# The scan's sums in fp16 high and low parts, and the group norm's centring in the summing matrix

## The reference, cut to what matters

```python
def step(S, inp):
    r_t, k_t, v_t, w_t = inp
    o_t = jnp.einsum('bhk,bhkv->bhv', r_t, S) + jnp.einsum('bhk,hk,bhk,bhv->bhv', r_t, u, k_t, v_t)
    S = jnp.exp(w_t)[..., None] * S + k_t[..., :, None] * v_t[..., None, :]
    return (S, o_t)
...
_, o = jax.lax.scan(step, S0, xs)
mean = o.mean(-1, keepdims=True)
var = o.var(-1, keepdims=True)
o = ((o - mean) * jax.lax.rsqrt(var + EPS)).reshape(B, T, VAL_DIM)
o = (o * gn_w + gn_b) * (g * jax.nn.sigmoid(g))
return o @ W_o
```

## Time and profile before

| | |
|---|---|
| median of 3 runs | 1851.65 us |
| lowest, highest | 1848.84, 1853.36 us |
| span of the profiled execution, first to last instruction | 1847.4 us |
| start of the scan's first product | 1714.6 us |
| start of the first gated product (L1738) | 1794.34 us |
| PE, DVE, ACT, POOL busy over the span | 94%, 78%, 76%, 77% |

### The profile page before, as it was taken

One profiled execution on the slowest core, in us unless ns is written; L12 is line 12 of the kernel. 1 busy time (PEld: TensorE's weight loads), 2 busy tenths in 40 slices (PEclk: granted clock), 3 DMA queues, 4 the chain that ended last, 5 costly groups with the idle time before them and its releaser, 6 DMA issues. The chain is left out here.

```text
span 1847.4 us, 53971 instructions
## 1 busy us (share of the span) xinstructions
PE 1740.1 (94%) x22856; PEld 1101.7 (60%) x22856; DVE 1444.6 (78%) x2658; ACT 1407.5 (76%) x1737; POOL 1430.4 (77%) x851
## 2 busy tenths in 40 slices
PE   5999999999999999999999999986899999978997
PEld 2466666666666666666666666675556666653454
DVE  5888888888888888888888887535988888845785
ACT  2688888888888888888888888943998888853463
POOL 6699999999999999999999999974765566624122
PEclk9899999999999999999999999998999999989998
DMA  5101010111101010101010010050111111110000
GB/s 142 25 20 31 19 31 23 27 26 28 26 24 30 21 31 19 31 23 28 23 31 23 24 26 4 2 165 18 41 40 36 37 37 37 34 26 1 1 0 24
DMA packets 71080, 56.89 MB, mean 31 GB/s; under 512 B 29196, under 2 KB 64184, under 8 KB 70840
## 3 DMA queue, kind: packets, MB, share of 16 engines
q1 hardware_dynamic: 70840, 53.44, 11.5%
HBM read 14.54 MB, written 1.05 MB: 8 GB/s over the span
## 5 line engine op out<-in xcount | busy, mean ns | idle before, releaser
L278 POOL TENSOR_TENSOR ah_probs_lo<-ah_probs,ah_probs_hi 128x1024 f16<-128x1024 f32 x512 | 1072.8, 2132 | 78.8 <-ACT ah_probs L487 78.7
L542 DVE TENSOR_REDUCE ah_part_max<-ah_p_m 128x1 f32<-128x512 f32 x1024 | 669.2, 685 | 120.9 <-PE ah_p_m L342 111.1
L484 ACT ACTIVATE ah_probs_hi<-ah_p_s 128x1024 f16<-128x1024 f32 x512 | 531.2, 1038 | 190.0 <-PE ah_p_s L358 178.8
L487 ACT ACTIVATE ah_probs<-ah_p_s 128x1024 f32<-128x1024 f32 x512 | 532.4, 1040 | 0.0
L372 PE MATMUL ah_p_o<-ah_v_hi,ah_probs_hi 128*128 128x65 f16 x4096 | 470.5, 195 | 5.7 <-POOL ah_probs_lo L278 5.1
L374 PE MATMUL ah_p_o<-ah_v_lo,ah_probs_hi 128*128 128x64 f16 x4096 | 470.5, 193 | 0.0
L376 PE MATMUL ah_p_o<-ah_v_hi,ah_probs_lo 128*128 128x65 f16 x4096 | 470.3, 194 | 0.0
L372 PEld LDWEIGHTS ah_p_o<-ah_v_hi,ah_probs_hi 128*128 128x128 f16 x4096 | 383.0, 98 | 84.3 <-DVE a_attn L565 12.3
L374 PEld LDWEIGHTS ah_p_o<-ah_v_lo,ah_probs_hi 128*128 128x128 f16 x4096 | 378.4, 98 | 91.3
L342 PE MATMUL ah_p_m<-ah_k_hi_lo,ah_q_hi_twice 128*128 128x512 f16 x1024 | 393.9, 385 | 6.6 <-DMA ah_max_q_lo<-ah_lo 3.1
L357 PE MATMUL ah_p_s<-ah_q_hi_twice,ah_k_hi_lo 128*128 128x512 f16 x1024 | 388.6, 379 | 0.8 <-ACT ah_probs L487 0.4
(11 more groups left out here) (316 smaller groups left out, 3090.0 us busy)
## 6 DMA issues: line engine op xcount, KB each, us to landing
ba_v_skew<-ba_v_own SPq DMA_DIRECT2D x64, 129.0 KB, 2.3
ah_q_hi_twice<-ah_hi SPq DMA_DIRECT2D x128, 64.0 KB, 2.0
ah_k_hi_lo<-ah_hi SPq DMA_DIRECT2D x64, 64.0 KB, 1.9
ah_one_k_hi<-ah_hi SPq DMA_DIRECT2D x64, 64.0 KB, 2.0
ah_k_hi_lo<-ah_lo SPq DMA_DIRECT2D x64, 64.0 KB, 2.0
ah_max_q_lo<-ah_lo SPq DMA_DIRECT2D x64, 64.0 KB, 2.0
ah_w_head<-in_w_heads SPq DMA_DIRECT2D x16, 160.0 KB, 2.4
bw_rot<-in_rot SPq DMA_DIRECT2D x4, 512.0 KB, 10.3
```

What stands on the lines that cost most here:

```text
L278: pool.tensor_tensor(pl[:, p % RW, :, :], pb[:, p % RP, :, :], ph[:, p % RW, :, :], ALU.subtract).then_inc(lo_pool, 1)
L484: act.activation(ph[:, p % RW, :, :], p_s[:, p % 2, :, :], ACT.Exp, scale=HD ** -0.5)
L487: act.activation(pb[:, p % RP, :, :], p_s[:, p % 2, :, :], ACT.Exp, scale=HD ** -0.5).then_inc(exp_done, 1)
L542: dve.tensor_reduce(part[:, t, 2 * half + b:2 * half + b + 1], p_m[:, b, :], AX, ALU.max).then_inc(maxed, 1)
```

## The change

`pr` is split for the sums: ACT writes its fp16 rounding `prh` (`pr_high`), POOL writes the fp16 rounding of the rest, `prl` = `pr` - `prh` (`pr_low`), and PE sums both in one PSUM accumulation with an fp16 matrix `selh`, eight matmuls of one pass where there were four fp32 ones. The summing matrix is no longer 0/1: its 8x8 blocks are 8I - 1, so the sums come out centred (and eight times too large, as before), and `centre` goes from DVE. ACT squares straight from PSUM and copies the centred values to SBUF for the norm. `out` runs two steps behind instead of one. POOL's queue is written step by step: a low part in every step, `gate_o` behind it at h = 0, `norm_o` at h = 2, `ln_root` at h = 3.

```diff
@@ phase_tail, tensor: out(n)
-                    pe.wait_ge(pr_done, n + 1)
+                    pe.wait_ge(prh_done, n + 1)
+                    pe.wait_ge(prl_done, n + 1)
                     if h == 0 and c >= 2:
                         pe.wait_ge(oc_done, c - 1)
+                        pe.wait_ge(squared, c - 1)
                     for t in range(TPC):
-                        mm = pe.matmul(p_o[:, c % 2, t * P + h * OC:t * P + (h + 1) * OC],
-                                       pr[:, n % 2, t * P:(t + 1) * P], sel[:, :], start=True, stop=True)
+                        o = p_o[:, c % 2, t * P + h * OC:t * P + (h + 1) * OC]
+                        pe.matmul(o, prh[:, n % 2, t * P:(t + 1) * P], selh[:, :], start=True, stop=False)
+                        mm = pe.matmul(o, prl[:, n % 2, t * P:(t + 1) * P], selh[:, :], start=False, stop=True)
                     mm.then_inc(o_ready, 1)
@@ the steps on tensor
-                    if n >= 1:
-                        out(n - 1)
+                    if n >= 2:
+                        out(n - 2)
...
+                out(STEPS - 2)
                 out(STEPS - 1)
@@ scalar
+                def pr_high(n):
+                    act.wait_ge(pr_done, n + 1)
+                    if n >= 2:
+                        act.wait_ge(o_ready, n - 1)
+                    act.activation(prh[:, n % 2, :], pr[:, n % 2, :], ACT.Copy).then_inc(prh_done, 1)
                 def square(c):
-                    act.wait_ge(oc_done, c + 1)
+                    act.wait_ge(o_ready, HCH * (c + 1))
                     if c >= 1:
                         act.wait_ge(ssq_done, c)
-                    act.activation(sq[:, :], oc[:, :], ACT.Square).then_inc(squared, 1)
+                        act.wait_ge(on_done, c)
+                    act.activation(sq[:, :], p_o[:, c % 2, :], ACT.Square).then_inc(squared, 1)
+                    act.activation(oc[:, :], p_o[:, c % 2, :], ACT.Copy).then_inc(oc_done, 1)
...
                     act.activation(v_sb[:, n % 2, :], p_v[:, :], ACT.Copy).then_inc(v_done, 1)
+                    if n >= 1:
+                        pr_high(n - 1)
                     if h == 0 and c == CLAST:
                         norm(1, 0)
...
+                pr_high(STEPS - 1)
                 norm(1, 1)
@@ gpsimd
+                def pr_low(n):
+                    pool.wait_ge(pr_done, n + 1)
+                    pool.wait_ge(prh_done, n + 1)
+                    if n >= 2:
+                        pool.wait_ge(o_ready, n - 1)
+                    pool.tensor_tensor(prl[:, n % 2, :], pr[:, n % 2, :], prh[:, n % 2, :],
+                                       ALU.subtract).then_inc(prl_done, 1)
...
-                for c in range(1, NCH):
-                    if c >= 2:
+                pool.wait_ge(late.scan_in, late.SCAN)
+                pool.tensor_copy(selh[:, :], sel[:, :]).then_inc(sel_done, 1)
+                for n in range(STEPS):
+                    c, h = divmod(n, HCH)
+                    pr_low(n)
+                    if h == 0 and c >= 2:
                         gate_o(c - 2)
-                    norm_o(c - 1)
-                    if c >= 2:
+                    if h == 2 and c >= 1:
+                        norm_o(c - 1)
+                    if h == 3 and c >= 2:
                         ln_root(1, c - 2)
@@ vector
-                def centre(c):
-                    dve.wait_ge(o_ready, HCH * (c + 1))
-                    dve.tensor_reduce(tot[:, :], heads(p_o[:, c % 2, :]), AX, ALU.add).then_inc(tot_done, 1)
-                    dve.wait_ge(tot_done, c + 1)
...
-                    dve.scalar_tensor_tensor(heads(oc[:, :]), heads(p_o[:, c % 2, :]), float(V_C),
-                                             tot[:, :].unsqueeze(2).to_broadcast([P, NG, V_C]), ALU.mult,
-                                             ALU.subtract).then_inc(oc_done, 1)
...
-                    if h == 1 and c >= 1:
-                        centre(c - 1)
...
                     if n >= 2:
-                        dve.wait_ge(o_ready, n - 1)
+                        dve.wait_ge(prh_done, n - 1)
+                        dve.wait_ge(prl_done, n - 1)
                     dve.tensor_tensor(pr[:, n % 2, :], m[:, n % 2, :], p_kr[:, 1, :], ALU.mult).then_inc(pr_done, 1)
...
-                centre(CLAST)
                 sum_squares(CLAST)
@@ the layout of the summing matrix
-    a["sel"] = c(np.eye(32, dtype=f).reshape(4, 1, 8, 32).repeat(4, 1).reshape(P, 32))
+    centred = np.kron(np.eye(4, dtype=f), vd * np.eye(vd, dtype=f) - 1)
+    a["sel"] = c(centred.reshape(4, 1, vd, 32).repeat(4, 1).reshape(P, 32))
```

More of the change, by code:

```diff
@@ L1579, in phase_tail @@
         pr = sc.sb("pr", [P, 2, CH])
-        tot = sc.sb("tot", [P, NG])
+        prh = sc.sb("pr_hi", [P, 2, CH], F16)
+        prl = sc.sb("pr_lo", [P, 2, CH], F16)
+        selh = sc.sb("sel_f16", [P, OC], F16)
         oc = sc.sb("centred", [P, CH])
@@ L1615, in phase_tail @@
          tw_ready, tw_done, g_ready, gth_done, gate_done, w_ready, v_ready, k_ready, r_ready, exp_done, dec_done,
-         v_done, kv_done, scanned, m_done, pr_done, o_ready, tot_done, oc_done, squared, ssq_done, std_done,
+         v_done, kv_done, scanned, m_done, pr_done, sel_done, prh_done, prl_done, o_ready, oc_done, squared, ssq_done, std_done,
          rstd_done, on_done, o_turned, tT_done, oT_done, y_ready, res_done, x2_turned, xT2_ready, gate_ready,
@@ L1622, in phase_tail @@
              "k_ready", "r_ready", "exp_done", "dec_done", "v_done", "kv_done", "scanned", "m_done", "pr_done",
-             "o_ready", "tot_done", "oc_done", "squared", "ssq_done", "std_done", "rstd_done", "on_done", "o_turned",
+             "sel_done", "prh_done", "prl_done", "o_ready", "oc_done", "squared", "ssq_done", "std_done", "rstd_done", "on_done", "o_turned",
              "tT_done", "oT_done", "y_ready", "res_done", "x2_turned", "xT2_ready", "gate_ready", "up_ready",
@@ L1748, in down @@
                         pe.wait_ge(oc_done, CLAST + c)
+                        pe.wait_ge(squared, CLAST + c)
                     for t in range(TPC):
@@ L1788, in _ @@
                 pe.wait_ge(consts, CONSTS)
+                pe.wait_ge(sel_done, 1)
                 pe.wait_ge(z_ready, NCH)
@@ L1997, in mix @@
                     pool.tensor_tensor(mixed_x, tmp[:, n % 2, :], xTp[:, xtok(c)], ALU.add).then_inc(mixed, 1)
+                def pr_low(n):
[5 more added lines that the diff above has]
+                                       ALU.subtract).then_inc(prl_done, 1)
                 def norm_o(c):
                     pool.wait_ge(rstd_done, c + 1)
+                    pool.wait_ge(oc_done, c + 1)
                     if c >= 1:
@@ L2072, in gate_g @@
                                              ALU.mult).then_inc(gate_done, 1)
-                def centre(c):
-                    dve.wait_ge(o_ready, HCH * (c + 1))
-                    dve.tensor_reduce(tot[:, :], heads(p_o[:, c % 2, :]), AX, ALU.add).then_inc(tot_done, 1)
-                    dve.wait_ge(tot_done, c + 1)
-                    if c >= 1:
-                        dve.wait_ge(on_done, c)
-                        dve.wait_ge(squared, c)
-                    dve.scalar_tensor_tensor(heads(oc[:, :]), heads(p_o[:, c % 2, :]), float(V_C),
-                                             tot[:, :].unsqueeze(2).to_broadcast([P, NG, V_C]), ALU.mult,
-                                             ALU.subtract).then_inc(oc_done, 1)
                 def sum_squares(c):
```

## The result

The changed kernel takes 1877.05 us, the median of 4 runs (1874.78 to 1878.2), against 1851.34 for the kernel before (4 runs, 1848.84 to 1853.36): ratio 1.0149, 95% interval 1.0132 to 1.0167. It is 25.7 us slower, where 20.5 were forecast. The profiled execution took 1877.33 us with a span of 1875.6, 28.2 more than before.

What follows compares the result with a forecast made beforehand. PE was taken to set the pace, by 0.8 us a step. Terms 0.2 + 8.0 + 6.7 + 5.6 made +20.5; 1847.4 + 20.5 + 4.3 = 1872.2 us, range 1865 to 1878.

Steps and rivals of the forecast that it cites:

- rival C: PE's waits in the scan lower its clock, each stretch costing about 3 us: +27, 1879 us; chance 0.12.
- What goes: Per scan step, eight short fp16 sums save PE 0.55 us; centring leaves DVE, 1.33 us per chunk.
- the loop: Scan steps with only the savings: kv, pr, sums and back to kv take 7.9 us for two steps, 3.95 each.
- One port: In scan steps POOL's low part and DVE's two-SBUF-input operations hold each other: +0.88 us per step, 3.50 becomes 4.38.
- The queues: Norm, gating and root wait behind low parts on POOL and high parts on ACT; such laps become 4.9 to 8.4 us.
- step 12: ACT's norm(1,0) waits for ln_root behind POOL's low part and the scan's hold: 8.4 us to the next kv.
- the way from kv(15): From the last kv to the first gated product: 7.2 us becomes 12.8, +5.6.
- the output step's terms: At h=1 of chunk 2, low part done at 2.95, gating 4.2, product 1.0, then 3.0 to kv: 8.1 us.
- root step with statistics: At h=2 where DVE also does reciprocal and statistics: 4.4 + 1.5, given as 5.8 us.
- Rival B: POOL does not hold DVE's 512-element operations in the scan, only queues cost: +12, 1863.7 us; chance 0.21.
- D: Queues do not bind, norm and gating start within 1 us of today: -2, 1849.7 us; chance 0.12.
- E: The fp16 sums on PE gain nothing because of weight changes, queues still bind: +20.5 to +22; chance within the forecast's 0.55.

Runs made afterwards that it cites:

- the third experiment: The changed kernel with useless fp32 products, their result overwritten, put where TensorE waits before norm transposes and output products: 1872.69 us, ratio 1.0118.

## Why the prediction was right, step by step

What happened is the forecast's two costs with rival C, the clock, on top. The port and the queues were right in place and nearly in size; the sum put the clock at nothing. That 1877.05 still lies in the range of 1865 to 1878 is in part luck: in the profiles 2.4 us came off behind the first gated product, where the forecast had 0, and without them the time would have lain above it.

- **What goes.** Right. Eight fp16 sums start between 1751.32 and 1751.49, 0.025 apart. The next product starts 0.20 after the first of them (in step 3), where it was 0.81: 0.61 saved per step for 0.55. Without the low part two plain laps are 7.70, for the 7.9 of the loop.
- **One port.** Right in place, nearly in size. Forecast was +0.88 on m, for a low part that comes after the scan's start. Where it does, the low part is held 0.91 and m takes 0.65 longer; in every other plain step the order is reversed and the scan is held 0.86 to 0.93. The plain laps of 4.31 to 4.43 bear out the 4.38. The prediction left open whether operations of 512 elements are held as the tiny ones were. They are, on both engines, and nearly for the whole of the other's instruction: a pair of 1.28 and 1.16 takes 2.23. The Trainium skill (SBUF — State Buffer, SBUF: two separate sides) says that whichever starts first gets the shared pair for the whole instruction and the other fully blocks; the trace agrees, with the second done 0.15 to 0.21 before the sum of both. What the step left out is that `norm_o` and `gate_o` are held too: 1.99 for 1.07 at the first norm step, and the gating 1714 in the mean for 1295 ns.
- **The queues.** Right, and by far the largest cost. The waits stood where they were put, though longer: before the transposes three times (3.30, 3.30, 3.36 for 2 to 3), before the output product twice (3.22, 6.78 for up to 5), ACT before norm(1,0) 4.67 for 3. Laps without PE waits came as forecast: 4.73 and 4.99 for 5.0 and 4.9, 5.52 and 5.75 for 5.8, 8.27 for 8.4. The way from kv(15) was 12.89 for 12.8. In step 12 two errors cancel: `ln_root` started before the scan had ended and not behind it, and its four operations then took 3.27 for 1.9 (1790.11 to 1793.38), so that it ended 4.84 after kv(12), where the forecast had 4.9.
- **The terms mis-sized** are the four laps with a wait of PE: 9.46, 10.20, 8.31 and 9.51 for 6.3, 8.1, 5.7 and 7.0, together 10.4 over. With the clock held up, 7.1 of them go. The rest, 3.3, is about what the held norm and gating give: 0.92 at each norm, 0.44 and 0.90 at the two gatings. The forecast's lap, the hold and the clock's share of the third experiment make 9.49, 10.14, 8.22 and 9.52, within 0.1 of what was measured.
- **Sums in the working.** Besides the loop two are out by 0.1: the output step's terms make 8.2 and not 8.1, those of the root step with statistics, counted twice, 5.9 and not 5.8; 0.3 in the sum. What lies around the span was taken as 4.3 us; each run's own span puts it at 1.7 to 1.8, and the rest was the profiled execution being faster than the median one. In the difference to the kernel before this term drops out.
- **Rival C**, the clock on top, was given 0.12 and happened: the sign named for it, products of the scan at 1.7 instead of 0.86, was there (starts 1.71 apart behind the first wait). Its 1879 was nearer to 1877 than the forecast's 1872. Its price of 3 us for each stretch was too high, and its two or three stretches inside the scan were four: 2.27, 1.60, 1.60 and 1.62. It was rated low because most of the new waits "stand between products that fill PE". The windows say that this does not protect: in the 18.03 us up to kv(7) PE was busy 16.50 us at a granted clock of 1.00, and one wait of 3.30 was enough. The Trainium skill (TensorE: Matmul & The Clock Gate, Part 1) has activity release the throttle and idleness bring it back; the trace agrees.
- **Rival B** (no port) falls by the stretched scans, **D** (queues do not bind) by the waits, **E** by the sums' times. Yet one moved line brought the queues to within 3.5 us of the kernel before.

## What to carry to other kernels

Work given to an idle engine is priced by what stands behind it in that engine's queue, not by the engine's idle time: 18.5 us on an engine that was 94% idle cost 25.7, and 24 of them were gone when the waited-for operations were put ahead of it. Look first for new waits of TensorE, and add to each the products behind it at half speed. A wait that was always there is worth the same look: the new order behind the last step made the way to the end 5 to 6 us shorter, with fp32 sums there. When DVE and GpSimd work side by side, give DVE's long operations one operand in PSUM, and see that this makes no new loop over the bank.
